# A four-layer sequence model on one core: where ScalarE changes its function tables in the state-space scan, softplus in pieces, and a weight split spread over two ticks

## The chip, the cores and the metric

One core of one Trainium2 chip runs the whole model in one launch. The metric is the device time of that launch in microseconds (us); less is better. The time before is the median of 3 runs.

## The reference

2048 tokens of width 512 pass four blocks. Each adds its result to x, and a layer norm over the 512 features follows.

1. Lightning attention: 16 heads, chunks of 128 tokens, per-head decay, gated group RMS norm.
2. Feed-forward: `hidden = silu(x @ W1.T) * (x @ W3.T)`, a Walsh-Hadamard transform over 2048 hidden features, `@ W2.T`.
3. A selective scan over the two sequences of 1024 tokens, 32 states for each of 512 features:

```
delta = softplus(dt + b_dt)
h = exp(delta_t * A) * h + (delta_t * u_t) * B_t
y_t = sum_n h * C_t + u_t * D_param
```

4. Feed-forward: `silu(gate) * up`, then `w_down`, again with 2048 hidden features.

What this case is about is the softplus of block 3, the inverse standard deviation of the layer norms, and the preparation of block 4's `w_down`.

## The kernel before, in words

Tokens lie along the free axis in 4 tiles (`NT`) of 512; features lie on 128 partitions in 4 groups (`KD`, index m). Every tile [128 x 512] is one "128x512" in the profile. After the attention comes `trunk_phase`: both feed-forwards, the scan and the norms. Its order is written out by hand. Time is cut into ticks from -24 to 791, and each engine (SyncE, which issues the DMAs, TensorE, ScalarE, VectorE, GpSimd) runs the same loop over ticks, asking tables such as `VAR_TICK`, `DT_TICK` and `PARTS_TICK` what falls due. An engine does its own list strictly in order and waits for the others by semaphores.

**Feed-forward.** Each tick holds one piece of TensorE work, 6 matmuls (`three_passes` at lines 111 to 113: weights and activations are split in a high and a low part, and three products are summed). 24 ticks make a unit of 4 hidden chunks. For each chunk ScalarE takes tanh of the gate half (line 1533), VectorE makes silu and the hidden value (1696, 1702), ScalarE and GpSimd split it in high and low (1537, 1831), and TensorE multiplies it down; VectorE adds the result to x (1708).

**Scan.** Ticks 118 to 653 carry 512 scan steps s, nearly one in each tick (tick 230 is one of those without a step). A step handles 32 states of 4 features on 128 partitions. In the tick of step s ScalarE makes the decay of step s+1 (`decay`, line 1630, an Exp of `delta_on_states` times A); it waits until the scan of step s-1 is done, because the decays have two buffers. VectorE runs the recurrence (`scan`, 1770) and multiplies the spread input by B (`d_b`, 1739 and 1747), GpSimd multiplies by C (1865) and makes one input in four (1856), and TensorE spreads (1455, waits for `d_b`) and sums states (1464). For each of the four token tiles the step sizes are made in the ticks before its scan: TensorE computes dt group by group (1423, `DT_TICK`), ScalarE takes |dt| and relu(dt) (`dt_take`, 1601 and 1602), and `soft` turns exp(-|dt|) into log(1 + ...):

```
act.activation(part, part, ACT.Exp, scale=-1.0)
act.preload_act_table_set(LOG_EXP)
act.activation(part, part, ACT.Ln, bias=1.0)
act.preload_act_table_set(EXP_TANH)
```

For tiles 1 to 3 that is one block over all four groups at once (128x2048), in ticks 230, 330 and 426 (lines 1607 to 1611). VectorE then adds (`step_size`, 1726) and multiplies by x (`step_input`, 1730).

**Two table sets.** ScalarE holds one set of functions at a time. `EXP_TANH` has exp and tanh, `LOG_EXP` has exp and log; `preload_act_table_set` is an ACT_TABLE_LOAD. The simple functions (copy, cast, square, abs, relu) run under either.

**Norms.** There are 14 (index e). TensorE sums the squares (1398 and 1404), and `inverse_root` at tick `VAR_TICK[e]` makes exp(-0.5 log(var + eps)) as: load LOG_EXP (1557), Ln (1559), Exp (1561), load EXP_TANH (1562). It stands in the tick behind that tick's `decay`. Norms 3 to 10 fall into the scan (ticks 212, 283, 308, 404, 465, 500, 551, 596).

**The down weights of block 4** are centred and split in 16 chunks, in `PRE_TICK`, 11 of them during the scan (every 22 ticks from 126). Three ticks after the load ScalarE does `pre_high`: a row mean (1523, two entries in the profile), centring (1525) and a cast to the high part (1527). GpSimd makes the low part (`pre_low`, 1827) a tick later, and SyncE stores both (`pre_store`) two ticks after that.

## Time and profile before

| | us |
|---|---|
| median of 3 runs | 1898.57 |
| lowest, highest | 1894.14, 1904.09 |
| the profiled execution's own time | 1897.86 |
| its span, first to last instruction | 1896.0 |

| engine | busy us | share of the span |
|---|---|---|
| TensorE (PE) | 1761.6 | 93% |
| VectorE (DVE) | 1328.4 | 70% |
| GpSimd (POOL) | 1285.5 | 68% |
| ScalarE (ACT) | 983.3 | 52% |

The 1.9 us between the span and the execution's own time lie around the instructions. The shares are means over stages that differ: the attention and the first norms take the first 550 us, the scan runs from 550 to 1707 us, and pure feed-forward ends the kernel. VectorE's 70% hides that it is busy for 93% of the scan.

### The profile page before, as it was taken

To read this page: it belongs to the slowest core of one execution; us is meant where nothing else is said; L and a number is where in the kernel's file an instruction comes from. 1 tells how busy PE (TensorE), PEld (TensorE's weight loads), DVE (VectorE), ACT (ScalarE), POOL (GpSimd) and SP (SyncE) were. 2 spreads that over 40 slices of the span, in tenths; PEclk is the share of its full clock that TensorE was granted. 3 is DMA by queue.
4 is the path that set the end of the run, shared out by engine and by line. 5 is a ranking of instruction groups with operands and counts; after the bars stand their busy time and mean duration, and the time that the engine had idled before them with its cause. 6 is when DMAs were issued, how large, how long until landed. Compare 5 with 4: busy or idle time off the path is not lost. (4 is left out here: it accounts for less than half of the span.)

```text
span 1896.0 us, 27444 instructions
## 1 busy us (share of the span) xinstructions
PE 1761.6 (93%) x9472; PEld 1152.8 (61%) x9472; DVE 1328.4 (70%) x1532; ACT 983.3 (52%) x1671; POOL 1285.5 (68%) x992
## 2 busy tenths in 40 slices
PE   7898998898998999989899899988999999999998
PEld 5566666576755565555555555555556555667886
DVE  2525344332259999799897999889999999994222
ACT  5344343566465656645566556556555655543212
POOL 4533445255449998688887998888889898883111
PEclk9999999999999999999999999999999999999999
DMA  7442332587668887678676887777678777874652
GB/s 244 129 144 74 123 105 97 184 304 269 242 215 277 290 297 254 211 265 289 226 252 230 291 283 257 230 243 248 230 264 280 253 258 260 278 265 157 209 191 97
DMA packets 159226, 427.32 MB, mean 225 GB/s; under 512 B 30992, under 2 KB 54096, under 8 KB 158704
## 3 DMA queue, kind: packets, MB, share of 16 engines
q1 hardware_dynamic: 159088, 425.57, 66.6%
q8 instruction: 76, 1.25, 0.3%
q14 instruction: 62, 0.51, 0.1%
HBM read 356.30 MB, written 69.21 MB: 224 GB/s over the span
## 5 line engine op out<-in xcount | busy, mean ns | idle before, releaser
L1630 ACT ACTIVATE decay<-delta_on_states,a_neg 128x512 f32<-128x512 f32 x512 | 354.2, 693 | 361.8 <-DVE h_states L1770 336.2
L1865 POOL TENSOR_TENSOR q_or_raw_or_h_times_c<-h_states,c_rep 128x512 f32<-128x512 f32 x293 | 382.0, 1316 | 63.9 <-PE scan_y L1464 34.3
L1865 POOL TENSOR_TENSOR h_times_c_rest<-h_states,c_rep 128x512 f32<-128x512 f32 x219 | 283.8, 1306 | 43.7 <-DVE h_states L1770 22.0
L1831 POOL TENSOR_TENSOR h_lo<-v_or_silu_in_h_lo,h_hi 128x512 fp32r<-128x512 f32 x128 | 167.9, 1312 | 205.4 <-ACT h_hi L1537 204.8
L1770 DVE TENSOR_TENSOR_SCAN h_states<-decay,h_last,d_b 128x512 f32<-128x512 f32 x192 | 243.2, 1281 | 9.2 <-ACT decay L1630 4.4
L1770 DVE TENSOR_TENSOR_SCAN h_states<-decay,d_b 128x512 f32<-128x512 f32 x192 | 231.4, 1216 | 14.8 <-ACT decay L1630 10.5
L111 PE MATMUL y_or_aux<-h_hi,w 128*128 128x512 f32 x468 | 208.2, 445 | 8.5 <-POOL h_lo L1831 5.2
L1455 PE MATMUL du_spread<-stack,selectors 96*128 96x512 bf16 x512 | 159.0, 389 | 48.8 <-DVE d_b L1739 22.5
L1696 DVE SCALAR_TENSOR_TENSOR v_or_silu_in_h_lo<-v_or_silu_in_h_lo,gate_or_scores 128x512 f32<-128x512 f32 x127 | 86.5, 681 | 147.7 <-ACT v_or_silu_in_h_lo L1533 147.3
L112 PE MATMUL y_or_aux<-h_lo,w 128*128 128x512 f32 x468 | 185.1, 395 | 0.0
L113 PE MATMUL y_or_aux<-h_hi,w 128*128 128x512 f32 x468 | 184.3, 394 | 0.0
L1856 POOL TENSOR_TENSOR d_b_by_pool<-du_copied,b_rep 128x512 f32<-128x512 f32 x128 | 171.4, 1339 | 8.6 <-ACT du_copied L1638 8.6
L1739 DVE TENSOR_TENSOR d_b<-du_spread,b_rep 128x1024 f32<-128x1024 f32 x128 | 154.3, 1206 | 10.4 <-PE du_spread L1455 9.8
L1464 PE MATMUL scan_y<-q_or_raw_or_h_times_c,sum_selectors 128*32 128x512 f32 x586 | 136.3, 611 | 0.0
L111 PEld LDWEIGHTS y_or_aux<-h_hi,w 128*128 128x128 f32 x468 | 89.1, 190 | 76.1 <-issue 36.0
L1537 ACT CAST h_hi<-v_or_silu_in_h_lo 128x512 fp32r<-128x512 f32 x128 | 78.7, 615 | 108.6 <-DVE v_or_silu_in_h_lo L1702 108.5
L1702 DVE SCALAR_TENSOR_TENSOR v_or_silu_in_h_lo<-v_or_silu_in_h_lo,up_or_scores 128x512 f32<-128x512 f32 x128 | 86.8, 678 | 64.3 <-PE up_or_scores L113 64.0
L1708 DVE TENSOR_TENSOR x<-x,y_or_aux 128x512 f32<-128x512 f32 x122 | 82.7, 678 | 67.9 <-PE y_or_aux L113 67.7
L111 PE MATMUL gate_or_scores<-attn_w_hi_or_x_hi_w 128*128 128x512 f32 x256 | 116.6, 455 | 9.4 <-DVE v_or_silu_in_h_lo L1696 8.2
L719 POOL TENSOR_TENSOR w_presplit_hi_lo<-w_presplit_hi_lo 128x512 fp32r<-128x512 f32 x32 | 41.4, 1316 | 114.9 <-ACT w_presplit_hi_lo L579 114.9
L111 PE MATMUL up_or_scores<-attn_w_hi_or_x_hi_w,attn_w_lo_or_x_lo_w 128*128 128x512 f32 x256 | 114.2, 446 | 2.5 <-DVE v_or_silu_in_h_lo L1702 2.5
L1464 PE MATMUL scan_y<-h_times_c_rest,sum_selectors 128*32 128x512 f32 x438 | 116.1, 609 | 0.0
(252 smaller groups left out, 4187.9 us busy)
## 6 DMA issues: line engine op xcount, KB each, us to landing
delta_on_states<-delta SPq DMA_DIRECT2D x256, 512.0 KB, 5.5
w<-w_split SPq DMA_DIRECT2D x112, 512.0 KB, 4.2
attn_w_hi_or_x_hi_w<-w_split SPq DMA_DIRECT2D x112, 512.0 KB, 4.1
attn_w_lo_or_x_lo_w<-w_split SPq DMA_DIRECT2D x112, 512.0 KB, 4.2
w_split<-w_presplit_hi_lo SPq DMA_DIRECT2D x32, 512.0 KB, 3.3
w_presplit_hi_lo<-in_w13b SPq DMA_DIRECT2D x32, 256.0 KB, 3.7
w_split<-attn_w_hi_or_x_hi_w SPq DMA_DIRECT2D x8, 1024.0 KB, 6.4
w_split<-attn_w_lo_or_x_lo_w SPq DMA_DIRECT2D x8, 1024.0 KB, 7.0
```

What stands on the lines that cost most here:

```text
L111: pe.matmul(out, w_hi, x_hi, start=first, stop=False)
L112: pe.matmul(out, w_hi, x_lo, start=False, stop=False)
L113: return pe.matmul(out, w_lo, x_hi, start=False, stop=last)
L1455: pe.matmul(uu[:, input_bank(s)], sel[:, r, :], stk[:, o % 2, j]).then_inc(s_uu, 1)
L1464: mm = pe.matmul(yb[j * 32:(j + 1) * 32, :], ysel[:, r, :], hc[(s + j) % NC_], start=(r == 0), stop=(r == QB - 1), skip_group_check=True, ...
L1630: act.activation(da[:, s % ND], dring[:, s % NR], ACT.Exp, scale=a[:, column(s):column(s) + 1]).then_inc(s_da, 1)
L1702: dve.scalar_tensor_tensor(out=sg[:, idx % RH], in0=sg[:, idx % RH], scalar=0.5, in1=up[:, :], op0=ALU.mult, op1=ALU.mult).then_inc(s_h, 1)
L1739: dve.tensor_tensor(db[:, :, :], uu[:, :, :], brep[:, tile_of(s // SPO) % 2].unsqueeze(1).to_broadcast([P, 2, TT]), ALU.mult).then_inc(s_d ...
L1770: dve.tensor_tensor_scan(hs[:, s % NH], da[:, s % ND], data, initial, ALU.mult, ALU.add).then_inc(s_hs, 1)
L1831: pool.tensor_tensor(hl[:, idx % RH], sg[:, idx % RH], hh[:, idx % RH].bitcast(F32), ALU.subtract).then_inc(s_hl, 1)
L1856: pool.tensor_tensor(dp[:, quad % 2], us[:, quad % 2], brep[:, tile_of(JB * quad // SPO) % 2], ALU.mult).then_inc(s_dp, 1)
L1865: pool.tensor_tensor(hc[s % NC_], hs[:, s % NH], crep[:, tile_of(s // SPO) % 2], ALU.mult).then_inc(s_hc, 1)
```

## The change

It touches ScalarE's list, and for the down weights GpSimd's and SyncE's.

- For tiles 1 to 3, `soft` is cut up. `soft_exp` of each group comes one tick behind its `dt_take`. `log_only` runs in three ticks: group 0, group 1, and groups 2 and 3 together (ticks 230 to 232, 331 to 333, 427 to 429). For tiles 2 and 3 the first log is one tick later than before. Tile 0 is as before.
- The table loads around them, and around the eight norms inside the scan, move to the head of a tick, ahead of that tick's `decay`: LOG_EXP at the head of the first tick with a log, EXP_TANH at the head of the tick behind the last one. For a norm these are `VAR_TICK[e]` and the next.
- `pre_high` is cut in two: mean and centring (`pre_centre`) stay, the cast moves to the next tick, and `pre_low` and `pre_store` follow one tick later.

```diff
--- before.py
+++ after.py
...
 STATES_TICK = ((114, 115), (233, 235), (330, 332), (426, 428))
-SOFT_TICK = (((108, (0,)), (114, (1, 2, 3))), ((230, (0, 1, 2, 3)),), ((330, (0, 1, 2, 3)),), ((426, (0, 1, 2, 3)),))
+SOFT_TICK = ((108, (0,)), (114, (1, 2, 3)))
+LOG_TICK = (None, 230, 331, 427)
 PARTS_TICK = ((109, 123, 131, 139), (231, 239, 247, 255), (332, 340, 348, 356), (428, 435, 442, 449))
...
     at_tick_by_m(PARTS_TICK, step) for step in range(8))
-SOFT_AT = {tick: (t_, ms) for t_, row in enumerate(SOFT_TICK) for tick, ms in row}
+SOFT_AT = {tick: (0, ms) for tick, ms in SOFT_TICK}
+EXP_AT = dict(SOFT_AT)
+EXP_AT.update({tick + 1: (t_, (m_,)) for tick, (t_, m_) in DT_AT.items() if t_})
+LOG_AT = {LOG_TICK[t_] + min(m_, 2): (t_, (2, 3) if m_ == 2 else (m_,)) for t_ in range(1, NT) for m_ in range(KD - 1)}
+NORM_IN_SCAN = [e for e, tick in enumerate(VAR_TICK) if SCAN_TICK <= tick < SCAN_TICK + SCAN_SPAN - 1]
+LOG_TABLE_AT = [VAR_TICK[e] for e in NORM_IN_SCAN] + [tick for tick in LOG_TICK if tick]
+TANH_TABLE_AT = [VAR_TICK[e] + 1 for e in NORM_IN_SCAN] + [tick + 3 for tick in LOG_TICK if tick]
 PRE_AT = at_tick(PRE_TICK)
...
                         w2_load(unit, m)
-                    if tick - 6 in PRE_AT:
-                        pre_store(PRE_AT[tick - 6])
+                    if tick - 7 in PRE_AT:
+                        pre_store(PRE_AT[tick - 7])
                     if tick in PRE_AT:
...
 
-                def pre_high(i):
+                def pre_centre(i):
                     act.wait_ge(s_bl, 16 * i + 16)
...
                     act.activation(pre[:, 0], pre[:, 0], ACT.Identity, bias=wmean[:, 2:3]).then_inc(s_bc2, 1)
+
+                def pre_high(i):
                     act.wait_ge(s_bc2, i + 1)
...
                 def inverse_root(e):
-                    if e not in AT_ONCE:
+                    if e not in AT_ONCE and e not in NORM_IN_SCAN:
                         act.preload_act_table_set(LOG_EXP)
...
                     act.activation(rstd[:, :], rstd[:, :], ACT.Exp, scale=-0.5).then_inc(s_r, 1)
-                    act.preload_act_table_set(EXP_TANH)
+                    if e not in NORM_IN_SCAN:
+                        act.preload_act_table_set(EXP_TANH)
 
...
 
-                def soft(t, ms):
+                def soft_exp(t, ms):
                     n, part = KD * t + ms[-1] + 1, soft_of(t)[:, ms[0]:ms[-1] + 1]
...
                     act.activation(part, part, ACT.Exp, scale=-1.0).then_inc(s_ex, len(ms))
+
+                def soft_log(t, ms):
+                    n, part = KD * t + ms[-1] + 1, soft_of(t)[:, ms[0]:ms[-1] + 1]
                     act.preload_act_table_set(LOG_EXP)
...
                     act.preload_act_table_set(EXP_TANH)
+
+                def log_only(t, ms):
+                    n, part = KD * t + ms[-1] + 1, soft_of(t)[:, ms[0]:ms[-1] + 1]
+                    act.wait_ge(s_ex, n)
+                    act.activation(part, part, ACT.Ln, bias=1.0).then_inc(s_so, len(ms))
 
...
                     s = step_at(tick)
+                    if tick in LOG_TABLE_AT:
+                        act.preload_act_table_set(LOG_EXP)
+                    if tick in TANH_TABLE_AT:
+                        act.preload_act_table_set(EXP_TANH)
                     if tick in W13_HIGH_AT:
...
                         w2_high(W2_HIGH_AT[tick])
+                    if tick in EXP_AT:
+                        soft_exp(*EXP_AT[tick])
                     if tick in SOFT_AT:
-                        soft(*SOFT_AT[tick])
+                        soft_log(*SOFT_AT[tick])
+                    if tick in LOG_AT:
+                        log_only(*LOG_AT[tick])
                     if tick in HIGH_AT:
...
                     if tick - 3 in PRE_AT:
-                        pre_high(PRE_AT[tick - 3])
+                        pre_centre(PRE_AT[tick - 3])
+                    if tick - 4 in PRE_AT:
+                        pre_high(PRE_AT[tick - 4])
 
...
                         part_low(*LOW_AT[tick])
-                    if tick - 4 in PRE_AT:
-                        pre_low(PRE_AT[tick - 4])
+                    if tick - 5 in PRE_AT:
+                        pre_low(PRE_AT[tick - 5])
 
...
```

ScalarE's list around ticks 330 to 334 (`soft_in_x_hi` holds exp(-|dt|) and its log), before, from the Exp of tick 330 on:

```order
L1607 ACTIVATE soft_in_x_hi<-soft_in_x_hi 128x2048
L1608 ACT_TABLE_LOAD
L1610 ACTIVATE soft_in_x_hi<-soft_in_x_hi 128x2048
L1611 ACT_TABLE_LOAD
L1630 ACTIVATE decay<-delta_on_states,a_neg 128x512 x2
L1595 COPY c_rep<-y_or_aux 128x512
L1630 ACTIVATE decay<-delta_on_states,a_neg 128x512
L1537 CAST h_hi<-v_or_silu_in_h_lo 128x512
```

and in the changed kernel, from the last Exp on, which stands in the same place:

```order
L1617 ACTIVATE soft_in_x_hi<-soft_in_x_hi 128x512
L1665 ACT_TABLE_LOAD
L1648 ACTIVATE decay<-delta_on_states,a_neg 128x512
L1629 ACTIVATE soft_in_x_hi<-soft_in_x_hi 128x512
L1648 ACTIVATE decay<-delta_on_states,a_neg 128x512
L1605 COPY c_rep<-y_or_aux 128x512
L1629 ACTIVATE soft_in_x_hi<-soft_in_x_hi 128x512
L1648 ACTIVATE decay<-delta_on_states,a_neg 128x512
L1546 CAST h_hi<-v_or_silu_in_h_lo 128x512
L1656 COPY du_copied<-du_spread 128x512
L1629 ACTIVATE soft_in_x_hi<-soft_in_x_hi 128x1024
L1667 ACT_TABLE_LOAD
```

One Exp, a load, one Ln and a load in a row have become an Exp of one group, a load, and three logs with a decay between each two; the second load stands ahead of the decay of tick 334. The other three Exp stand earlier in the list.

ScalarE's list at ticks 283 and 284, where norm 4 and a down-weight chunk meet, before:

```order
L1630 ACTIVATE decay<-delta_on_states,a_neg 128x512
L1557 ACT_TABLE_LOAD
L1559 ACTIVATE rstd<-y_or_aux,sum_weights_eps 128x512
L1561 ACTIVATE rstd<-rstd 128x512
L1562 ACT_TABLE_LOAD
L1638 COPY du_copied<-du_spread 128x512
L1585 CAST attn_w_hi_or_x_hi_w<-x 128x512
L1523 ACTIVATE w_presplit,minus_w_mean<-w_presplit 128x4x128
L1525 ACTIVATE w_presplit<-w_presplit,minus_w_mean 128x512
L1527 CAST w_presplit<-w_presplit 128x4x128
L1630 ACTIVATE decay<-delta_on_states,a_neg 128x512
```

and in the changed kernel:

```order
L1665 ACT_TABLE_LOAD
L1648 ACTIVATE decay<-delta_on_states,a_neg 128x512
L1568 ACTIVATE rstd<-y_or_aux,sum_weights_eps 128x512
L1570 ACTIVATE rstd<-rstd 128x512
L1656 COPY du_copied<-du_spread 128x512
L1595 CAST attn_w_hi_or_x_hi_w<-x 128x512
L1530 ACTIVATE w_presplit,minus_w_mean<-w_presplit 128x4x128
L1532 ACTIVATE w_presplit<-w_presplit,minus_w_mean 128x512
L1667 ACT_TABLE_LOAD
L1648 ACTIVATE decay<-delta_on_states,a_neg 128x512
L1595 CAST attn_w_hi_or_x_hi_w<-x 128x512
L1536 CAST w_presplit<-w_presplit 128x4x128
```

The first load has passed the decay of tick 283. The second has moved behind the centring of the down weights (L1532), still ahead of the decay of tick 284, and the cast (L1536) has moved behind that decay.

## Rows read from the trace of the kernel before

**Rows 1.** Busy time by stretch: us, engines (instructions), granted clock, DMA share, GB/s
```profile
550.00:1707.00 1157.00, 1088.40 (x4897) 661.80 (x4896) 1074.05 (x1122) 661.96 (x1163) 1005.45 (x788) 0.99 0.77 260
1010.00:1030.00 20.00, 20.00 (x82) 10.74 (x82) 13.61 (x15) 17.12 (x23) 13.93 (x12) 1.00 0.76 252
1030.00:1097.00 67.00, 57.16 (x260) 34.84 (x259) 66.21 (x68) 36.02 (x61) 60.56 (x47) 1.00 0.82 269
1240.00:1278.00 38.00, 31.54 (x144) 18.98 (x143) 37.60 (x39) 19.53 (x40) 34.25 (x27) 1.00 0.79 255
```

**Rows 2.** Waits of the whole run: us in total, times, longest us
```profile
ACT decay L1630 <- DVE h_states L1770: 336.2, 301, 5.8
...
DVE h_states L1770 <- ACT decay L1630: 24.4, 15, 4.2
```

**Rows 3.** ScalarE in order of time, tick 330: start, us, what, [idle before]
```profile
1022.95 1.91 ACT L1607 ACTIVATE soft_in_x_hi<-soft_in_x_hi 128x2048 f32<-128x2048 f32 x1
1024.88 1.28 ACT L1608 ACT_TABLE_LOAD   x1
1026.17 1.91 ACT L1610 ACTIVATE soft_in_x_hi<-soft_in_x_hi 128x2048 f32<-128x2048 f32 x1
1028.10 1.28 ACT L1611 ACT_TABLE_LOAD   x1
1029.40 1.30 ACT L1630 ACTIVATE decay<-delta_on_states,a_neg 128x512 f32<-128x512 f32 x2
```

**Rows 4.** VectorE behind ticks 330 and 426
```profile
1030.12 1.28 DVE L1770 TENSOR_TENSOR_SCAN h_states<-decay,h_last,d_b 128x512 f32<-128x512 f32 x1 [4.03 <-ACT decay L1630]
...
1038.10 1.27 DVE L1770 TENSOR_TENSOR_SCAN h_states<-decay,h_last,d_b_by_pool 128x512 f32<-128x512 f32 x1
...
1240.03 1.22 DVE L1770 TENSOR_TENSOR_SCAN h_states<-decay,d_b 128x512 f32<-128x512 f32 x1 [4.18 <-ACT decay L1630]
```

**Rows 5.** VectorE behind tick 230
```profile
789.07 0.69 DVE L1726 TENSOR_TENSOR delta_in_x_lo<-delta_in_x_lo,soft_in_x_hi 128x512 f32<-128x512 f32 x1 [1.74 <-ACT soft_in_x_hi L1610]
791.07 1.22 DVE L1770 TENSOR_TENSOR_SCAN h_states<-decay,d_b 128x512 f32<-128x512 f32 x1 [1.31 <-ACT decay L1630]
...
798.29 0.69 DVE L1696 SCALAR_TENSOR_TENSOR v_or_silu_in_h_lo<-v_or_silu_in_h_lo,gate_or_scores 128x512 f32<-128x512 f32 x1 [1.79 <-ACT v_or_silu_in_h_lo L1533]
```

**Rows 6.** TensorE behind tick 230, in order of time
```profile
792.92 1.84 PE L1419 MATMUL y_or_aux<-mean_or_rank,w_dt_state_selectors 32*128 32x512 f32 x2 [2.40 <-DVE x L1708]
```

**Rows 7.** The 10 us around it, columns as in Rows 1
```profile
790.00:800.00 10.00, 7.59 (x18) 4.19 (x16) 7.06 (x8) 6.42 (x13) 8.35 (x7) 0.66 0.54 169
```

**Rows 8.** TensorE behind tick 330
```profile
1026.51 1.12 PE L1419 MATMUL y_or_aux<-mean_or_rank,w_dt_state_selectors 32*128 32x512 f32 x2
...
1032.13 0.47 PE L111 MATMUL up_or_scores<-attn_w_hi_or_x_hi_w,attn_w_lo_or_x_lo_w 128*128 128x512 f32 x1 [1.09 <-DVE v_or_silu_in_h_lo L1702]
```

**Rows 9.** ScalarE, groups by shape: x count | busy us, mean ns | idle before
```profile
L1607 ACT ACTIVATE soft_in_x_hi<-soft_in_x_hi 128x512 f32<-128x512 f32 x1 | 0.6, 633 | 0.0
```

**Rows 10.** ScalarE at tick 308
```profile
968.40 0.69 ACT L1630 ACTIVATE decay<-delta_on_states,a_neg 128x512 f32<-128x512 f32 x1 [1.43 <-DVE h_states L1770]
969.11 1.28 ACT L1557 ACT_TABLE_LOAD   x1
970.40 0.69 ACT L1559 ACTIVATE rstd<-y_or_aux,sum_weights_eps 128x512 f32<-128x512 f32 x1
```

**Rows 11.** TensorE at tick 308
```profile
969.04 1.02 PE L1404 MATMUL y_or_aux<-rstd,sum_weights_eps 128*128 128x512 f32 x2
```

**Rows 12.** ScalarE at tick 283
```profile
911.88 0.70 ACT L1630 ACTIVATE decay<-delta_on_states,a_neg 128x512 f32<-128x512 f32 x1
...
919.07 0.62 ACT L1527 CAST w_presplit<-w_presplit 128x512 fp32r<-128x512 f32 x1
```

**Rows 13.** VectorE at tick 283
```profile
914.07 1.28 DVE L1770 TENSOR_TENSOR_SCAN h_states<-decay,h_last,d_b 128x512 f32<-128x512 f32 x1
...
920.32 1.28 DVE L1770 TENSOR_TENSOR_SCAN h_states<-decay,h_last,d_b_by_pool 128x512 f32<-128x512 f32 x1 [3.79 <-ACT decay L1630]
```

## The prediction

> **What bounds the kernel now.** I read the table of busy times by stretch first. In the scan (550 to 1707 us) TensorE is busy for 1088 of 1157 us and VectorE for 1074 [rows 1]; ScalarE has 662. So two engines are nearly full and take turns in setting the pace, and ScalarE sets it only where it is late with a decay. The waits say how often: ScalarE stands 336.2 us before decays, waiting for the scan, while VectorE waits for a decay for 24.4 us, in 15 places [rows 2]. That second number, and not ScalarE's busy time, is the size of what this change can reach.
>
> The timelines then show where it lies. At tick 330 ScalarE makes an Exp over four groups, a load, an Ln and a load in a row, from 1022.95 to 1029.40, and only then the next decay [rows 3]. VectorE stands still for 4.03 us before the scan that needs it; at tick 426 for 4.18 us [rows 4]. At tick 230 it is 1.74 us for the logs and 1.31 us for the decay [rows 5]. Together 11.3 us.
>
> Is such a stop lost, or made up? Ahead of the block of tick 330 TensorE sets the pace: from 1010 to 1030 it is busy for 20.00 of 20 us, VectorE for 13.61. Behind it VectorE does: 66.21 of 67 us, while TensorE has 9.8 us of idle time. Behind tick 426 it is 37.60 of 38 us against 6.5 us of idle TensorE [rows 1]. VectorE makes up nothing there, so what it does not stand still it ends earlier, as long as TensorE's idle time (9.8 and 6.5 us) is more than the stop (4.0 and 4.2 us), and it is.
>
> **Part 1: softplus in pieces.** I lay the new list of tick 330 on the old times. The Exp of the last group takes 0.63 us [rows 9] from 1022.95, to 1023.6. The load takes 1.28 [rows 3], to 1024.9, the decay 0.69 [rows 10], to 1025.6. VectorE is ready for it at 1030.12 - 4.03 = 1026.09 [rows 4]: it no longer waits. The first Ln (0.63) ends at 1026.2 and the next decay at 1026.9. The copy of C must wait for TensorE, 1026.51 + 1.12 = 1027.63 [rows 8]; with 0.6 for it, 0.63 for the second Ln and 0.69 for the decay it is 1029.6. Two short copies of 0.6, the last Ln and the load follow. For an Ln over two groups the trace has no row: it lies between 0.63 (one group, [rows 9]) and 1.91 (four, [rows 3]), and a straight line gives 1.06. So 1029.6 + 1.2 + 1.06 + 1.28 = 1033.1, and the fourth decay is done at 1033.8. VectorE needs it for the scan that now starts at 1038.10 and would start at 1034.1 [rows 4]. All four come in time, the last by 0.3 us; with the Ln at 1.91 it would be 0.6 late. Gain 4.0 us, at least 3.4. What is late next is TensorE's copy of C (0.9 us for ScalarE, inside the slack).
>
> At tick 426 list and times are alike: **4.0 us** again, of 4.18, and I book **4.0** for tick 330. At tick 230 the head of the tick has no decay behind it, since there is no step, so the load is free. VectorE saves 1.74 + 1.31 = 3.05 us, the least value. There is more: TensorE stood for 2.40 us because VectorE's addition came late [rows 6], and its granted clock then went from 2.4 to 1.2 GHz: the mean over 790 to 800 us is 0.66, or 3.4 us of work lost [rows 7], and VectorE waited another 1.79 us for a tanh that this held up [rows 5]. TensorE had come to that matmul at 792.92 - 2.40 = 790.5; the addition, done at 792.9, would be done 3.05 us earlier, at 789.8. So 2.40 + 3.4 = **5.8 us** if the clock stays up, 3.05 if it falls all the same. I take 5.8, since the idle time that preceded the fall goes.
>
> Added work: four Exp of 0.63 instead of one of 1.92 and three Ln instead of one make 0.6 + 0.4 = 1.0 us of ScalarE for each tile, 3 us in all, and three of the four Exp stand where dt is made. The 336 us before decays [rows 2] cover them: 0. Without cover it would be 9 x 0.63 = 5.7 us.
>
> **Part 2: loads at the head of the tick, eight norms.** At tick 308 ScalarE waits 1.43 us before its decay, so a load of 1.28 ahead of it is free, and the Ln could start at 969.11 instead of 970.40 [rows 10]. But it needs TensorE's sum, done at 969.04 + 1.02 = 970.06 [rows 11]: 0.3 us gained, not 1.28. The second load moves too, but not off the chain: ScalarE is late there, and the load still stands ahead of the next decay. At tick 283 there is no wait before the decay; it would end at 911.88 + 1.28 + 0.70 = 913.9, and VectorE takes it at 914.07 [rows 12, 13]: just free. Its stop of 3.79 us [rows 13] shrinks by the cast alone, 0.6 us. All eight norms: at best 8 x 0.3 = +2.4 us, at worst two places where the load is not covered, 2 x 1.28 = -2.6; both are guesses from these two norms, and I take 0, between them.
>
> How much a load costs is itself in question. In the trace the decay at tick 308 ends at 969.09, the load starts at 969.11 and the Ln at 970.40: 1.3 us in all [rows 10]. The Trainium skill, in "ScalarE: Activation LUTs", What ACT_TABLE_LOAD costs, gives a load of 1283 ns and with it a drain of about 1380 ns, 2.66 us for every switch to another set. By that, an estimate from the page, each of the eight first loads would stick out by up to 1.38 us from a wait of about 1.3 us, 11 us in all, and the sum would be 1896 instead of 1885. This trace agrees with the load to the nanosecond and shows no drain behind or ahead of it.
>
> **Part 3: the down weights.** The cast (0.62, [rows 12]) leaves a group of four in a row, 11 times; no new work. GpSimd's subtraction and SyncE's store move a tick back, past a C product or a load of step sizes, each ready before. The next chunk comes 22 ticks later, so nobody waits for them. 0, or 0.6 where it meets a norm.
>
> **Sum.** 4.0 + 4.0 + 5.8 = 13.8 us. The profiled execution took 1897.9 us and would take 1884.1; the median of the runs before is 0.7 higher, 1898.6, which gives **1885** (1884.8).
>
> **The rivals.**
>
> *TensorE takes the gain (25%).* It is full for the 20 us ahead of the block, and it has run nearly full for the scan as a whole (94%). If it is TensorE that sets the pace behind the blocks too once VectorE no longer lags, only its own idle time that a stop causes is won: 2.40 at tick 230 [rows 6], 1.09 at tick 330 [rows 8], as much at tick 426, so 4.6 us: **1894**. Against it: 9.8 and 6.5 us of idle TensorE behind the blocks.
>
> *The clock gives more (12%).* If fewer stops also spare TensorE the fall of its clock elsewhere, each fall of the size of [rows 7] is worth 3.4 us. Two more of them give **1878**. For it: the granted clock averages 0.99 over the scan [rows 1], so some 12 us are lost to falls in all. Against: the stops of 4 us at ticks 330 and 426 were followed by none, the clock is 1.00 there [rows 1].
>
> *The loads stand in the decay's way (7%).* One mechanism with the opposite sign: in ten of the eleven places a decay now waits behind a load of 1.28 us that stood behind it. If ScalarE is late in those ticks for the dt work, 10 x 1.28 = 12.8 us are added to VectorE's path, the nine Exp among the dt ticks add 5.7, and the stops only move from one tick to four: 1898.6 + 18.5 = **1917**. It decides where VectorE's slack for a decay is under 1.28 us; at tick 283 it is just enough [rows 12, 13], at tick 308 the wait of 1.43 covers the load [rows 10]. Since both places that I looked at cover it, it gets 7%. The drain of the page named above would feed the same mechanism: with 2.66 us for a load it would cost 26.6 us instead of 12.8.
>
> *The change does not do what it says.* Exp is in both sets, so the decays of ticks 230 to 233 need no reload, and the new list has as many loads as the old. No tanh falls under the log set. I give it nothing.
>
> **How the numbers follow.** The forecast has 56%; with TensorE 25%, clock 12%, loads 7%. A measurement of this kernel tells 0.5%, 9.5 us, from no change. Forecast and clock lie beyond it, 68% faster; TensorE's case is no change, 25%; the loads' case is slower, 7%. The range goes from 1877 (the clock's case, 1 us of norms) to 1896 (TensorE's case, 2 us lost at norms); it holds the forecast's own bounds, 13.8 less 2.8 for the clock and 0.6 for the Ln, and leaves out the loads' case.
>
> **What the profile after would show.** Right: VectorE's wait for a decay falls from 24.4 us to about 12, with no wait over 1 us at ticks 230 to 234, 330 to 334 and 426 to 430; the 2.40 us of TensorE at tick 230 and the low clock behind it are gone; ScalarE's total is 3 us higher; the stop at tick 283 stays near 3 us. Wrong: the waits go as said and the time hardly moves (TensorE's case, to be seen as VectorE's waits for tanh and for 1702 growing by as much); or VectorE's waits for decays are more in number, behind the new loads.

## The result and the profile after

Before: 1895.34 us (median of 5 runs beside the change, 1893.73 to 1904.09). After: **1877.42 us** (5 runs, 1876.29 to 1881.10). The ratio is 0.9901, with an interval of 0.9883 to 0.9919: faster by 18.8 us (15.4 to 22.2), against the 13.8 of my sum. Later medians of the kernel before were 1895.4 to 1898.6, and the change measured again gave 1876.91, 0.9909 [0.9894, 0.9923], 17.3 us. From here on a ratio is the time by that of the kernel before, with its interval in square brackets. The direction was right and the size too small.

The waits of the changed kernel, in us, number and longest, answer to [rows 2]:

```profile
ACT decay L1648 <- DVE h_states L1798: 328.5, 294, 5.4
...
DVE h_states L1798 <- ACT decay L1648: 9.9, 10, 3.1
```

VectorE waits 9.9 us for decays in place of 24.4 (12.6 in a second execution of the change, 21.8 and 24.4 in two more of the kernel before). The windows of the scan and of block 230 (ticks 227 to 236) after, columns as in [rows 1]:

```profile
547.70:1686.60 1138.90, 1083.00 (x4897) 660.29 (x4896) 1075.79 (x1121) 660.73 (x1177) 1004.92 (x787) 0.99 0.79 264
774.90:794.80 19.90, 19.90 (x84) 11.27 (x84) 17.14 (x19) 15.54 (x28) 15.48 (x12) 1.00 0.72 245
```

and the same block before:

```profile
777.50:802.00 24.50, 22.09 (x75) 12.58 (x76) 16.80 (x20) 15.90 (x23) 15.27 (x12) 0.86 0.62 212
```

The scan takes 1138.9 us in place of 1157.0. In block 230 TensorE's 2.40 us of idle time and the fall of its clock to 1.2 GHz behind it (granted clock 0.86 over the block) are gone: it is busy from end to end at 1.00. ScalarE's list at tick 330, which answers to [rows 3]:

```profile
1012.11 0.63 ACT L1617 ACTIVATE soft_in_x_hi<-soft_in_x_hi 128x512 f32<-128x512 f32 x1
1012.76 1.28 ACT L1665 ACT_TABLE_LOAD   x1
1014.06 0.69 ACT L1648 ACTIVATE decay<-delta_on_states,a_neg 128x512 f32<-128x512 f32 x1
1014.69 0.61 ACT L1629 ACTIVATE soft_in_x_hi<-soft_in_x_hi 128x512 f32<-128x512 f32 x1
...
1019.45 1.07 ACT L1629 ACTIVATE soft_in_x_hi<-soft_in_x_hi 128x1024 f32<-128x1024 f32 x1
1020.53 1.28 ACT L1667 ACT_TABLE_LOAD   x1
1021.83 0.69 ACT L1648 ACTIVATE decay<-delta_on_states,a_neg 128x512 f32<-128x512 f32 x1
1022.45 0.58 ACT L1542 ACTIVATE v_or_silu_in_h_lo<-gate_or_scores 128x512 f32<-128x512 f32 x1
```

and VectorE there, which answers to [rows 4]:

```profile
1020.98 1.27 DVE L1798 TENSOR_TENSOR_SCAN h_states<-decay,h_last,d_b 128x512 f32<-128x512 f32 x1
1023.07 0.69 DVE L1724 SCALAR_TENSOR_TENSOR v_or_silu_in_h_lo<-v_or_silu_in_h_lo,gate_or_scores 128x512 f32<-128x512 f32 x1 [0.81 <-ACT v_or_silu_in_h_lo L1542]
```

No scan waits for its decay. The last piece and the load behind it instead make the **tanh** of line 1542 late, by 0.81 us: I had looked at the decays alone. At tick 426 the tanh is late by 0.93.

### The profile page after: what moved, and what is told of

It reads as the page before. It is cut to its first block and busy times, and to the rows that moved or that the text cites. A ratio compares the mean times of both kernels' runs of the same rounds, so it can differ in the third digit from the quotient of the medians.

```text
span 1875.5 us, 27456 instructions
## 1 busy us (share of the span) xinstructions
PE 1755.9 (94%) x9472; PEld 1150.7 (61%) x9472; DVE 1329.8 (71%) x1532; ACT 981.9 (52%) x1686; POOL 1285.6 (69%) x992
## 3 DMA queue, kind: packets, MB, share of 16 engines
q8 instruction: 76, 1.25, 0.3%
## 5 line engine op out<-in xcount | busy, mean ns | idle before, releaser
L1462 PE MATMUL du_spread<-stack,selectors 96*128 96x512 bf16 x512 | 157.9, 389 | 41.8 <-DVE d_b L1775 18.9
L111 PE MATMUL gate_or_scores<-attn_w_hi_or_x_hi_w,attn_w_lo_or_x_lo_w 128*128 128x512 f32 x256 | 115.6, 452 | 0.5 <-DVE v_or_silu_in_h_lo L1724 0.5
```

Source lines behind the costliest of these rows:

```text
L111: pe.matmul(out, w_hi, x_hi, start=first, stop=False)
L1462: pe.matmul(uu[:, input_bank(s)], sel[:, r, :], stk[:, o % 2, j]).then_inc(s_uu, 1)
```

## Where the time went, with its scatter

One profile of each kernel would have misled me here. This table has the length in us of stretches between the starts of scans, of three executions of the kernel before, two of the change, and two with softplus in pieces alone (experiments below). Some stretches overlap:

```
ticks     before (three)        change (two)   pieces alone (two)
0-118     550.4 549.3 551.0     547.7 549.7    549.3 549.7
118-211   186.4 189.1 187.5     186.7 187.9    189.2 188.4
211-227    40.7  40.7  40.7      40.6  40.6     42.8  42.8
227-236    24.5  24.4  23.1      19.9  19.9     20.0  19.9
227-240    35.4  35.3  33.7      29.7  29.7     29.7  29.7
236-252    41.8  38.0  37.6      40.6  36.8     36.8  40.6
252-278    57.6  55.9  55.9      56.0  55.7     55.9  56.4
278-286    22.5  24.1  22.5      21.9  21.9     24.0  24.1
328-336    24.8  24.8  24.8      21.2  21.2     21.2  21.2
328-344    40.8  42.0  40.8      36.7  36.7     37.0  36.7
336-361    55.0  55.9  53.4      54.4  54.4     58.6  58.1
420-428    22.9  22.9  22.9      18.8  18.8     18.8  18.8
420-441    51.2  51.3  52.3      47.9  47.9     47.9  47.9
546-562    36.9  36.9  36.9      37.8  37.8     37.0  37.0
span     1896.0 1892.6 1888.5  1875.5 1874.2  1884.1 1887.6
```

The three blocks are where the pieces gain: up to ticks 236, 336 and 428 about 4.1 (from a mean of 24.0), 3.6 and 4.1, 11.8 us. Apart from block 230 before they repeat to 0.1 us. Where a stage is cut matters, though. VectorE still stands 1.4 us behind block 230 before, in tick 236 to 237, and in the change the late tanh behind block 426 takes 0.7 us of its gain back. Followed until the difference stops changing from tick to tick, to ticks 240, 344 and 441, the gains are 5.1, 4.5 and 3.7 us against the mean of the three executions before, **13.3 us**. Block 230 gives 5.7 in the two executions where the fall of the clock has its full length, and 4.0 in the third.

Other stages differ by 4 us between executions of one kernel. The means of the spans are 1892.4 and 1874.9, 17.5 apart, so 4.2 us lie outside the blocks.

## The experiments

All edits are against the changed kernel and shown in part; `...` stands for lines left out.

**Softplus in pieces alone**, norms and down weights as before, twice:

```diff
-LOG_TABLE_AT = [VAR_TICK[e] for e in NORM_IN_SCAN] + [tick for tick in LOG_TICK if tick]
+LOG_TABLE_AT = [tick for tick in LOG_TICK if tick]
...
-                    if tick - 4 in PRE_AT:
-                        pre_high(PRE_AT[tick - 4])
+                    if tick - 3 in PRE_AT:
+                        pre_high(PRE_AT[tick - 3])
```

> Only the softplus in pieces; the loads of the norms and the down weights as before. Theory A (the blocks carry the change): 14 us under before (14.1 us fell away at the three blocks in the profile of the change), about 1881 to 1884, VectorE's wait for decays near 12 us, and up to the scan the same times as before. Theory B (the pieces are worth only VectorE's own stops, 11.3 us, and the clock at tick 230 is luck): 8 to 11 us. Theory C (the gain is mostly the loads at the heads of the ticks of the norms and the earlier down weights): under 8 us.

> The softplus in pieces alone, again: it measured 8.7 us under the kernel before (5.7 to 12), where my sum had 13.8. Theory A (the part is worth what its three blocks gain, 12 us, and the rest was scatter of the clock): ratio .992 to .994, low clock under 50 us, and no loss of 3.6 at ticks 336 to 361. Theory B (the low clock stretches behind block 330 belong to this order without the spread of the down weights): the same two stretches near 1064 and 1084, ratio .995 to .996.

Measured 0.9954 [0.9937, 0.9970] and 0.9947 [0.9931, 0.9962]: 8.7 and 10.0 us, with the blocks as in the change. VectorE's waits for decays are 16.4 and 13.1 us, for the "near 12" expected. The second came between its two theories: 3.1 us are lost again at ticks 336 to 361, with one low stretch of TensorE's clock, at 1088, in place of two. So the other parts are worth 7 to 10 us beside it. Stage 211 to 227 says where a part of that is: it is 2.1 us longer than in any execution before. Of the 2.1 us between these two and the change at 278 to 286, only 0.7 are the cast; the other 1.5 come at tick 283, with a low stretch of the clock at ticks 281 to 283 that one of the three executions before shows too. ScalarE at tick 217 without the spread of the down weights:

```profile
757.94 0.65 ACT L1616 ACTIVATE soft_in_x_hi<-soft_in_x_hi 128x512 f32<-128x512 f32 x1
758.48 0.63 ACT L1530 ACTIVATE w_presplit<-w_presplit 128x512 f32<-128x512 f32 x1
...
759.99 0.62 ACT L1536 CAST w_presplit<-w_presplit 128x512 fp32r<-128x512 f32 x1
760.51 0.69 ACT L1647 ACTIVATE decay<-delta_on_states,a_neg 128x512 f32<-128x512 f32 x1
761.14 0.58 ACT L1542 ACTIVATE v_or_silu_in_h_lo<-gate_or_scores 128x512 f32<-128x512 f32 x1
```

and in the change:

```profile
753.83 0.64 ACT L1617 ACTIVATE soft_in_x_hi<-soft_in_x_hi 128x512 f32<-128x512 f32 x1
754.36 0.63 ACT L1530 ACTIVATE w_presplit<-w_presplit 128x512 f32<-128x512 f32 x1
...
755.74 0.67 ACT L1648 ACTIVATE decay<-delta_on_states,a_neg 128x512 f32<-128x512 f32 x1
756.35 0.58 ACT L1542 ACTIVATE v_or_silu_in_h_lo<-gate_or_scores 128x512 f32<-128x512 f32 x1
756.83 0.61 ACT L1536 CAST w_presplit<-w_presplit 128x512 fp32r<-128x512 f32 x1
```

The new Exp (0.65) falls on the tick of a down-weight chunk, ahead of a late tanh. Alone it makes the tanh later: VectorE waits 1.94 us for it in place of 1.43, TensorE then 1.63 for VectorE in place of 1.11, and its clock falls at 767.1 in both executions, and in no other of the eighteen profiles in these ticks. VectorE's stop behind it, for TensorE's spread of the inputs, grows from 1.0 to 2.6 us (2.3 in the second). In the change the cast has left just that place. The pieces need the spread of the down weights here.

**Down weights alone**, with softplus as before, and the same with everything behind their load a tick later still (centre, cast, subtraction, store 4, 5, 6, 8 ticks behind it in place of 3, 4, 5, 7):

```diff
-LOG_TICK = (None, 230, 331, 427)
+LOG_TICK = ()
...
 SOFT_AT = {tick: (0, ms) for tick, ms in SOFT_TICK}
+SOFT_AT.update({230: (1, (0, 1, 2, 3)), 330: (2, (0, 1, 2, 3)), 426: (3, (0, 1, 2, 3))})
```

> Only the down weights over two ticks. Theory A with what the profile of the change showed ahead of the scan: 2 to 4 us under before, nearly all ahead of tick 118, because ScalarE's tanh no longer stands behind the cast of a chunk whose load came late (TensorE's stop there 3.5 instead of 5.5 us, and one low stretch of the clock 3.4 instead of 6.8 us); within the scan 0.6 at tick 283. Rival (those 2.4 us ahead of the scan are scatter of the DMA): within 1 us of before, and the stop of 5 us behind the late load still there.

> The kernel before with the down weights spread alone, centring and all a tick later still; softplus and norms as before. Theory A (the spread of the down weights is worth 3 to 5 us by itself, and the late centring 3 more, because ScalarE's list does not stop behind a late load): 1887 to 1890, ratio .9950 to .9970, with VectorE's waits for a decay still near 24 us, ScalarE's waits for that load under 6 us in place of 16.7, and TensorE's stop near 464 gone. Theory B (the 4.6 us of the cast alone were the scatter of TensorE's clock, and the late centring's 3 us too): 1894 to 1896, ratio over .9985, with the stages as before but for the clock.

Measured 0.9976 [0.9961, 0.9991], 4.6 us, and 1888.52, 0.9956 [0.9939, 0.9973], 8.3 us. The second is as its first theory had it. The first gains more than the 2 to 4 us expected, and its one profile, which is of the slowest of its ten executions, does not show them "nearly all ahead of tick 118": TensorE's stop behind the late transfer there is 3.14 us in place of 5.45, with a low stretch of 3.4 in place of 6.8, but ticks 0 to 118 take 549.4. In the scan ticks 219 and 285 come 0.7 us earlier each, about the length of the cast. I had booked 0.

**Pieces and down weights without the norms' loads**, and **the norms' loads alone**:

> The changed kernel without the moved loads of the norms. If these are worth what their own stretches show (0.3 us at tick 308, 0.5 at 404, minus 0.9 at 551): within 1 us of the changed kernel, about 1877 to 1879. If loads and pieces help each other, since the parts alone gave 9.5, -0.9 and 3.5 us and all three together 18: 4 to 6 us slower, about 1883.

> Only the loads around the eight norms moved to the heads of the ticks. Theory A: 0 to 1.5 us under before (the profile of the change shows 0.4 at tick 308, 0.5 at 404, 0 at the others), since the log waits for TensorE's sum anyway and the second load stays in the chain; the stops at ticks 213 and 405 stay at 1.1 us. Theory C: 4 us or more. The loads in the way of the decays: slower by up to 4 us, with new stops before scans at ticks 283, 551 and 465.

Measured 0.9908 [0.9884, 0.9932] and 1.0008 [0.9994, 1.0021]. The norms' loads are worth nothing that these runs can tell from 0 (-4.0 to +1.1 us alone), as booked: 0.3 us at tick 308, which is the booked figure, 0.5 at 404, and 0.9 lost at ticks 546 to 562. ScalarE at tick 308 after, where the load ends early and the Ln waits 1.25 us for TensorE's sum all the same:

```profile
956.36 1.28 ACT L1665 ACT_TABLE_LOAD   x1
957.66 0.69 ACT L1648 ACTIVATE decay<-delta_on_states,a_neg 128x512 f32<-128x512 f32 x1
959.60 0.69 ACT L1568 ACTIVATE rstd<-y_or_aux,sum_weights_eps 128x512 f32<-128x512 f32 x1 [1.25 <-PE y_or_aux L1411]
```

**One Exp over four groups**, in the tick of the last dt:

```diff
-EXP_AT.update({tick + 1: (t_, (m_,)) for tick, (t_, m_) in DT_AT.items() if t_})
+EXP_AT.update({DT_TICK[t_][-1] + 1: (t_, (0, 1, 2, 3)) for t_ in range(1, NT)})
```

> The changed kernel, but the four Exp of a tile are one again, in the place of the last of them; the logs and the loads stay in pieces. If the pieces of the Exp are what keeps the decays in time: 1.3 us more of ScalarE in front of the first load, of which VectorE's slack at tick 331 covers 0.5, so 0.8 us for each of three tiles and 2 to 3 us slower than the changed kernel. If the decays between the logs alone do it: no more than 1 us slower.

Measured 0.9935 [0.9920, 0.9950], 12.3 us: 5.0 to 6.5 us slower than the change, outside both expectations. Ticks 227 to 240 take 32.2 us, 328 to 344 take 38.9 and 420 to 441 take 48.4, which is 2.5, 2.3 and 0.5 more than in the change. So in this profile 5.3 of the blocks' 13.3 us hang on the Exp's pieces, and 8.0 on the Ln's pieces and the early load. Part of the 5.3 comes a few ticks behind the blocks, where VectorE's additions of a step size at ticks 239 and 340 take 3.38 and 2.64 us in place of 1.77 and 0.86 (more on these below).

**The tanh table loaded ahead of the next tanh only**, and **two loads ahead of each norm's decay** (one more for the price of a load, 8 x 1.28 = 10.2 us if each stuck out; the first of the two loads the set that ScalarE already holds):

```diff
+def next_tanh(tick):
+    return min(t for t in TANH_AT if t >= tick)
-TANH_TABLE_AT = [VAR_TICK[e] + 1 for e in NORM_IN_SCAN] + [tick + 3 for tick in LOG_TICK if tick]
+TANH_TABLE_AT = [next_tanh(VAR_TICK[e] + 1) for e in NORM_IN_SCAN] + [next_tanh(tick + 3) for tick in LOG_TICK if tick]
```

```diff
                     if tick in LOG_TABLE_AT:
+                        if tick in VAR_AT:
+                            act.preload_act_table_set(EXP_TANH)
                         act.preload_act_table_set(LOG_EXP)
```

> The changed kernel, but the load of the tanh set waits until the head of the next tick that has a tanh (ticks 214, 286, 310, 406, 466, 502, 554, 598; at the blocks 234, 334, 430), instead of the tick behind the norm. If the second load is still in the chain to a late decay, as forecast: the stops of VectorE before a scan at ticks 213 and 405 (1.14 us each), the one of 3.13 at 284 (less 1.28) and those of 0.68 and 0.41 behind ticks 500 and 596 go, 4.6 us in all, and the time falls 3 to 5 us below the changed kernel, about 1873. If those stops are due to Ln, Exp and copies alone: within 1 us of the changed kernel.

> The changed kernel with a second load ahead of the decay at the eight norm ticks, 8 x 1.28 = 10.3 us more of ScalarE. If the wait of ScalarE before the decay and VectorE's slack cover about 2.5 us, as the rows of ticks 212 and 308 say: 1.3 us at tick 283, where there is no wait, some tenths at 308, 465 and 551, 2 to 3 us slower than the changed kernel. If a load ahead of a decay is on VectorE's path (the rival of the prediction that ended slower): 8 to 10 us slower. If each load brings a drain of 1.38 us with it: 20 us more ScalarE, over 10 us slower, and gaps of that size behind or ahead of loads in the timeline.

The late load: 0.9900 [0.9877, 0.9923], no different from the change, though VectorE's waits for decays fall to 4.1 us. The stops at ticks 213, 405, 500 and 596 that it removes lie where TensorE is full, and their stages keep their length within 0.2 us; 278 to 286 gains 1.4. Block 230 loses 1.3 up to tick 236, where the tanh now stands behind the load and VectorE waits 1.86 us for it in place of 0.53, and has made it up by tick 240; 0.5 is lost at tick 311. The doubled loads: 0.9924 [0.9902, 0.9946], 3 to 4.5 us worse than the change, of which the stages show 1.3 at ticks 278 to 286 and the rest as scatter. The pair of loads at tick 308:

```profile
960.15 1.28 ACT L1666 ACT_TABLE_LOAD   x1
961.44 1.28 ACT L1667 ACT_TABLE_LOAD   x1
962.74 0.69 ACT L1648 ACTIVATE decay<-delta_on_states,a_neg 128x512 f32<-128x512 f32 x1
```

1.29 us from start to start, and 1.30 from the second load to the decay: no drain shows beside the 1.28 of a load, neither behind the load of a set already held nor behind the one that changes the set.

**The centring a tick later in the change**, with cast, subtraction and store each a tick later too:

```diff
...
-                    if tick - 3 in PRE_AT:
-                        pre_centre(PRE_AT[tick - 3])
                     if tick - 4 in PRE_AT:
-                        pre_high(PRE_AT[tick - 4])
+                        pre_centre(PRE_AT[tick - 4])
+                    if tick - 5 in PRE_AT:
+                        pre_high(PRE_AT[tick - 5])
...
```

> The changed kernel with the whole of the down weights' work (mean, centring, cast, low part, store) one more tick after the load. If a late load blocks ScalarE's list ahead of the scan and the tanh behind it: ScalarE's waits for the chunk's load fall from 19.8 us to under 10, TensorE's stop of 3.5 us at 463 us goes, and the scan starts 2 to 4 us earlier; in the scan the stop at tick 284 falls by about 1.5 us. Together 3 to 5 us below the changed kernel. If the scan's start is ruled by something else: within 1 us ahead of the scan.

Measured 1875.02 (1874.06 to 1875.78), 0.9883 [0.9867, 0.9899]; all four runs lie below all nine of the change. It shows what the spread of the down weights does ahead of the scan. In the change ScalarE stands at a chunk whose transfer is late, with a tanh queued behind it:

```profile
460.97 0.63 ACT L1530 ACTIVATE w_presplit<-w_presplit 128x512 f32<-128x512 f32 x1 [4.49 <-DMA w_presplit<-in_w2b]
...
462.36 0.58 ACT L1542 ACTIVATE v_or_silu_in_h_lo<-gate_or_scores 128x512 f32<-128x512 f32 x1
```

TensorE then stops for 3.53 us and its clock falls at 463, for 3.4 us. In the kernel before ScalarE's wait is 5.75 us, TensorE's stop 5.45 and the low stretch 6.8. A tick later the transfer has nearly landed, and the tanh stands ahead of it:

```profile
458.57 0.60 ACT L1542 ACTIVATE v_or_silu_in_h_lo<-gate_or_scores 128x512 f32<-128x512 f32 x1 [1.10 <-PE gate_or_scores L113]
459.99 0.63 ACT L1530 ACTIVATE w_presplit<-w_presplit 128x512 f32<-128x512 f32 x1 [0.82 <-DMA w_presplit<-in_w2b]
```

ScalarE's waits for these transfers fall from 19.8 us to 3.7. TensorE's stop there is 2.05 us, at 468 and now behind GpSimd's low part of the hidden value, no fall of the clock is near it, and ticks 211 to 227 and 278 to 286 gain 1.1 and 1.4.

All eighteen profiles agree on this stop: 5.3 to 5.8 us in the six without the spread of the down weights, 3.0 to 3.6 in the eight with it, 1.9 to 2.1 in the four with the later centring. The low stretch there is 6.8 us in five of the six (3.4 in one), 3.4 in the eight, none in the four. Ticks 0 to 118 are shorter by less than that on the average: 549.4, 548.3 and 545.3 us.

**Both later edits together**, and **the change again**:

> The change with both edits that each did no harm: the down weights' centring, cast, subtraction and store a tick later still, and the tanh table loaded ahead of the next tanh only. The first alone measured 22 us under the kernel before, the second 19, the change 19. Theory A (stops that reach TensorE are what is left to win, and the tanh load's stops lie where TensorE is full): the second edit adds at most the 1.4 us that it won at ticks 278 to 286 where the first won as much, so nothing: 1872 to 1876, ratio .987 to .989. Theory B (each late decay costs its stop): 5.8 us of waits for a decay gone, so 1868 to 1870, ratio under .987.

> The changed kernel again, unedited, for the spread of its time and of where TensorE's clock falls. Theory A (clock falls other than the one at tick 230 come by scatter): time within 1876 to 1881, low clock between 25 and 55 us in all in place of 42.1, at other places than before, the one at tick 230 absent again, VectorE's waits for a decay at 9.9 us within 0.5. Theory B (the falls are fixed by the order of the work): the same places as in the first profile.

Together 0.9891 [0.9869, 0.9912], 1874.0: no gain beyond the first edit that shows, as the first theory said. The change again: 1876.9, low stretches of 35.2 us in all with none at tick 230, the waits for decays 12.6 us, not within 0.5 of 9.9, and ticks 236 to 252 in 36.8 us in place of 40.6. That last difference has a cause that none of my theories held. VectorE's addition of a step size at tick 247, in the first execution of the change:

```profile
821.28 5.24 DVE L1754 TENSOR_TENSOR delta_in_x_lo<-delta_in_x_lo,soft_in_x_hi 128x512 f32<-128x512 f32 x1
826.45 1.21 DVE L1798 TENSOR_TENSOR_SCAN h_states<-decay,d_b 128x512 f32<-128x512 f32 x1
```

beside GpSimd in that execution:

```profile
819.70 2.55 POOL L1893 TENSOR_TENSOR q_or_raw_or_h_times_c<-h_states,c_rep 128x512 f32<-128x512 f32 x2
822.18 1.31 POOL L1859 TENSOR_TENSOR h_lo<-v_or_silu_in_h_lo,h_hi 128x512 fp32r<-128x512 f32 x1
823.42 1.32 POOL L1893 TENSOR_TENSOR h_times_c_rest<-h_states,c_rep 128x512 f32<-128x512 f32 x1
824.66 1.31 POOL L1884 TENSOR_TENSOR d_b_by_pool<-du_copied,b_rep 128x512 f32<-128x512 f32 x1
```

and the same addition in the second execution, with one a little later that takes an operand from TensorE's bank:

```profile
824.44 1.59 DVE L1754 TENSOR_TENSOR delta_in_x_lo<-delta_in_x_lo,soft_in_x_hi 128x512 f32<-128x512 f32 x1
...
827.09 0.66 DVE L1736 TENSOR_TENSOR x<-x,y_or_aux 128x512 f32<-128x512 f32 x1
```

with GpSimd beside it:

```profile
822.94 2.55 POOL L1893 TENSOR_TENSOR q_or_raw_or_h_times_c<-h_states,c_rep 128x512 f32<-128x512 f32 x2
825.43 1.75 POOL L1859 TENSOR_TENSOR h_lo<-v_or_silu_in_h_lo,h_hi 128x512 fp32r<-128x512 f32 x1
827.14 1.30 POOL L1893 TENSOR_TENSOR h_times_c_rest<-h_states,c_rep 128x512 f32<-128x512 f32 x1
```

In the first it ends 0.5 us behind the last of GpSimd's back-to-back instructions (824.66 + 1.31 = 825.97, against 826.5). In the second it ends behind the first two of them, after 1.59 us, and it is GpSimd's h_lo that takes 1.75 us in place of 1.31. Of the sixteen additions of an execution none to three took over 3 us, nineteen in the eighteen profiles. Each of the nineteen lies on a row of GpSimd instructions without a gap, and ends 0.55 us behind the end of one of them. Ticks 236 to 252 are 35.5 to 38.4 us where the one at 247 is short and 40.6 to 41.8 where it is long; 336 to 361 are 58 in both executions of the pieces alone, where the one at 356 took 5.60 and 5.16, and 54.4 in the change, where it took 1.62 and 1.48. TensorE pays behind it, here in the pieces alone, at half the clock:

```profile
1084.60 1.03 PE L1462 MATMUL du_spread<-stack,selectors 96*128 96x512 bf16 x2 [4.80 <-DVE d_b L1774]
```

The Trainium skill, in "SBUF — State Buffer", Who interferes with whom, has a rule for this: a VectorE instruction with both inputs in SBUF and a GpSimd instruction that reads SBUF contend for a shared port, which the page calls an exclusive lock. The trace agrees: this addition reads both from SBUF, while x<-x,y_or_aux took its 0.66 us beside a busy GpSimd. So do all eighteen profiles, over the scan: the element-wise 128x512 operations of VectorE whose two inputs both lie in SBUF vary (this addition from 0.66 to 5.85 us, three others from about 0.67 to 1.8), while each form with an operand in TensorE's banks keeps within 0.07. What the traces show beyond the page's rule is that VectorE can lose the turn several times in a row: at tick 247 it stood behind the instruction under way and three more, in the 5.60 of the pieces alone behind four more.

**GpSimd leaves a gap**, in the change and in the version with the later centring:

```diff
+                    if tick in SIZE_AT:
+                        t, m = SIZE_AT[tick]
+                        pool.wait_ge(s_de, KD * t + m + 1)
                     if tick in H_SPLIT_AT:
                         h_low(H_SPLIT_AT[tick])
```

> The change, and GpSimd waits, in each of the sixteen ticks in which VectorE adds a step size, for that addition, before its next subtraction. In the executions so far the addition took about 0.7 to 1.9 us or, in none to three of its sixteen places, 3.4 to 5.9; each long one lay on a stretch in which GpSimd went from instruction to instruction without a gap, and cost its stage 3.7 to 4.6 us. Theory A (VectorE's addition is held off by GpSimd's instructions, several in a row if they leave no gap, and that is the scatter between executions): with the wait no addition is over 2 us, ticks 236 to 252 gain 5.0 us against before, ticks 336 to 361 do not lose, and the median falls by 2 to 5 us from the change's 1877 to 1872 to 1875. Theory B (the long ones come from something else, such as the fetch of instructions or a transfer): long additions stay as frequent, and the time is the change's 1877 or, with GpSimd held up, 1878 to 1880.

> The same wait on GpSimd in the change with the down weights' centring a tick later (which measured 1875.0 and had one long addition, of 5.33 us at tick 247). Theory A: no addition over 2 us, 1870 to 1872, the lowest of all. Theory B: 1875 to 1877.

In the first, GpSimd and VectorE at tick 247:

```profile
827.17 1.29 POOL L1859 TENSOR_TENSOR h_lo<-v_or_silu_in_h_lo,h_hi 128x512 fp32r<-128x512 f32 x1 [0.63 <-DVE delta_in_x_lo L1754]
```

```profile
825.47 1.62 DVE L1754 TENSOR_TENSOR delta_in_x_lo<-delta_in_x_lo,soft_in_x_hi 128x512 f32<-128x512 f32 x1
```

The addition runs in the forced gap, and of the sixteen none takes over 1.8 us; ticks 236 to 252 take 37.2, 336 to 361 53.8. In the second two take 2.90 and 2.57: there GpSimd had two instructions ahead of its wait, and the addition ran as soon as they were done. So the delay ends with GpSimd's row of instructions, as the contention has it; that no addition is long in one forced execution would not show it alone, since three of the sixteen profiles without this wait have none over 3 us either. The theory's time is not borne out: 1877.3, 0.9900 [0.9883, 0.9917], is no less than the change, and 1873.5 (1871.32 to 1875.82), 0.9881 [0.9865, 0.9897], is no clear gain over 1875.0. Whether the executions without a profile have fewer long additions, or GpSimd's wait costs what it saves, stays open.

**The kernel before, twice more**:

> The kernel before, unedited, profiled again, as the control for every stage that I compare with it. So far one execution of it stands against fourteen of its relatives. Theory A (part of the change's surplus over my sum was chance in that one execution): some of the stages in which all the others are faster whatever they edit (ticks 252 to 278 by 1.5 us, 462 to 479 by 1.2) are faster here too, and ticks 236 to 252 by 3.8 if the addition at tick 247 is short. Theory B (the order before is itself worse there): these stages agree with the first profile within 0.3 us. In both the waits at ticks 330 and 426 (4.03 and 4.18 us) and the 2.40 us of TensorE at tick 230 with the low clock behind it stay.

> The same once more. Theory A: these stages scatter again, one way or the other, by 1 to 4 us in ticks 236 to 278; the three blocks agree within 0.2 us. Theory B: every stage of the scan agrees with the first profile within 0.3 us.

The medians are 1897.24 and 1895.36, 0.9999 [0.9976, 1.0022] and 0.9996 [0.9979, 1.0013]. The spans of the profiled executions are 1892.6 and 1888.5, and ticks 236 to 252 and 252 to 278 are shorter by 3.8 to 4.2 and by 1.7: chance, as theory A had it. The first profile was at the long end of both. The stops of the blocks are the same each time, and so is the fall of the clock at tick 230, though once at half its length (3.4 us in place of 6.8), which makes that block 23.1.

## Why the prediction was wrong in its size

- **What bounds it: right.** What VectorE does not stand still ends earlier at all three blocks, and the blocks take the same time in both executions of the change and both of the pieces alone, within 0.3 us. TensorE's case (1894), 4.6 us in all, is out.
- **Part 1: 13.8 booked, 13.3 measured, right.** Block 230 gave 5.7 us for 5.8 where the clock had fallen for its full 6.8 us, and 4.0 where it fell for 3.4, so TensorE's 2.40 and the 3.4 of lost work are both won. Block 330 gave 4.1 to 5.4 and block 426 3.3 to 4.4 for the 4.0 booked for each. The late tanh, which I had not looked at, leaves 3.6 and 3.4 of the 4.0; at tick 340 a step-size addition of VectorE that is 0.87 us long in place of 1.39 to 2.65 adds 0.5 to 1.8, which I had not foreseen either. That the sum comes so close is in part luck.
- **Added work at 0: right only with Part 3.** The rows of Exp and Ln of the softplus sum to 18.8 us in place of 15.7, the 3 us said. All of ScalarE's instructions sum to 1057.1 us in place of 1054.4. The page's busy total did not rise (981.9 for 983.3), since it counts the overlap of neighbours once. But the "336 us before decays" is no cover at tick 217, where the list is full ahead of a late tanh: there the pieces alone cost 2.1 us.
- **Part 2 at 0: right**, to the 0.3 us of tick 308. The sum by the drain that the Trainium skill has in "ScalarE: Activation LUTs", What ACT_TABLE_LOAD costs, 1896, was out: from a load to the next instruction the traces show 1.29 to 1.30 us. The stop at tick 283 stays, 3.13 us for the "near 3" said.
- **Part 3 at 0: this is the step that failed.** "The next chunk comes 22 ticks later, so nobody waits for them" looked behind the cast only, and inside the scan only. The cast stood ahead of a decay or a tanh in ScalarE's list: at ticks 217 and 283 in the scan, 0.7 us each (for 283 I had named 0.6, and booked 0), and ahead of the scan, where most chunks come 8 ticks apart and transfers are late; there TensorE's stop fell from 5.45 to 3.14 us. It measured 4.6 us (1.7 to 7.4) alone, and, with the norms' loads that add nothing, 7 to 10 us beside the pieces. Added to what Part 1 gave, 13.3 + 4.6 = 17.9 us, against 17.3 to 18.8 measured for the whole.
- **The clock's case (1878) has the nearest number, by luck.** TensorE's granted clock averages 0.9871 over the 19 executions of the kernel before beside its second measurement, and 0.9899 over nine of the change. That is 0.0129 x 1894.6 = 24.4 against 0.0101 x 1875 = 18.9 us of work lost, 5.5 fewer, of which I had booked 3.4; the case wanted 6.8 beyond those, and 2.1 came. The pieces alone average 0.9862 beside 0.9861 of the kernel before and 0.9879 beside 0.9871, the down weights alone 0.9880 beside 0.9861 and, with the later centring, 0.9898 beside 0.9871. So it is the spread of the down weights, more than the pieces, that keeps the clock up. The single Exp, with 0.9870 beside 0.9861, falls out of that line. Single falls elsewhere move from execution to execution.

Left open: how the gain outside the blocks divides among stages that scatter by up to 4 us, and why the pieces alone, which gain 13.3 us at the blocks and lose 2.1 at tick 217, end at 8.7 and 10.0. Only medians of several runs give these a size.

## What to carry to other kernels

An instruction that moves to the next tick is worth what stands behind it in its engine's list when that list is late, so look at the places where moved and added work meet, and not at the engine's mean slack. Take a second and third profile of the kernel before ahead of reading a stage's difference as an effect: here stages of 40 us differ by 4 between executions, while others repeat to 0.1. And move the end of a stage a few ticks on before you book its difference: block 230 gained 4.5 us up to tick 236 and 5.7 up to tick 240. If an engine's list stops at a late transfer, put what others wait for ahead of it: one tick more for the chunk took 2 us off the change by the medians (3.4 to 4.9 by the ratios), and the three versions with it, 1873.5 to 1875.0, are the fastest measured here.

## What the hardware showed that I had not expected

- The same 128x512 addition of VectorE took 0.66 to 5.85 us, by how GpSimd's instructions beside it follow each other; the lost 3.7 us and TensorE's low clock behind it are much of what tells two executions of one kernel apart in a stage.
- TensorE's low stretches are 3.4 or 6.8 us long (4.3 to 7.4 the one with which each run ends), here and there by chance, but at tick 230 in each of six profiled executions with the old softplus and in none of twelve with the new.
- Two table loads in a row take 1.28 us each, with 0.01 between them, also where the first loads the set already held.
